# Graph attention and mixture-of-experts block on one core: new places in the instruction queues for the first softmax tiles, and a turn of 33 places

## The chip, the cores and the metric

The kernel runs on one NeuronCore of a Trainium2 chip. The metric is the device time of one execution in microseconds (us). Before the change the median of 3 runs is 1457.65 us (1455.25 to 1458.83); the execution that was profiled took 1455.44 us, of which the span from its first to its last instruction is 1453.6 us.

## The reference

The reference adds to a node table x (1250 x 768, float32) first a two-layer graph attention network of layernorm(x), then a transformer block with 12-head attention and a top-2 mixture of 8 experts. The change lies in graph attention layer 1:

```python
h = x @ W
e_src = h @ a_src
e_dst = h @ a_dst
e = leaky_relu(e_src[src] + e_dst[dst], 0.2)
m = segment_max(e, dst)
w = exp(e - m[dst])
z = segment_sum(w, dst)
out = segment_sum(h[src] * (w / z[dst])[:, None], dst) + b      # then relu, then layer 2
```

There are 41,250 edges (20,000 drawn, each in both directions, and the 1250 self-loops), sorted by dst.

## The kernel before

**Dense form of the graph.** The 1250 nodes are T = 10 tiles of 125. For each destination tile the kernel counts how many edges run from each source to each destination (a 125 x 1250 table `cnt`), and the segment sums become matrix products. The counts come from one-hot matrices: 38 steps per tile, 380 in all. In step g TensorE multiplies a destination one-hot by a source one-hot (`step_near`, L1960). VectorE makes the source one-hots in batches of 4 steps (2 at a tile's end; `ohs`, L2403) and the destination one-hots in batches of 12 or 14 (`ohd`, L2337); ScalarE scales each destination one-hot by a packed power (`valued`, L2102). After 38 steps ScalarE copies the counts out (`counted`, L2089) and VectorE unpacks them (`unpacked`, L2416). Steps of the next tile that use the same PSUM bank wait for that copy.

**Layer 1's products.** For each tile t, in float32 split into high and low parts: transpose (`transposes1`, L1914), ScalarE's high part (`higher1`, L2072), VectorE's low part (`lower1`, L2363), twelve triples of matrix products (`triple1`, L457 to L459), the result's high part (`result1` on ScalarE, L2083), the scores (`score1` on VectorE, L2374) and the result's low part (`rest1`, L2379). The source scores go through DRAM to be spread over all partitions (`esb`): the first 8 tiles' scores in one transfer, the last 2 tiles' in a second.

**The softmax of tile t.** ScalarE turns the counts into a mask (`distant`, L863). VectorE takes the masked maximum (`far_max`, L880; for tile 0 in two parts, L903), forms the shift (`shift_sum` L885, `shift` L889) and adds and clips the scores (`leaky`, L896; for tile 0 in two parts, L900). ScalarE's `sloped1` (L800) makes the 0.2-scaled scores `es02` that the clip reads, in the same two parts. ScalarE takes the exponential (`exponential`, L849), VectorE multiplies by the counts (`weigh`, L909), TensorE transposes (`turned`, L811), ScalarE copies out the high part (`higher`, L854, L855), VectorE the low part (`lower`, L914, L915), and TensorE does 20 triples (`triple_sum`, L457 to L459). `ending` (L919, L2388) divides and adds the bias.

**The order is written out.** Every engine takes its instructions strictly in its own queue's order. The queue of layer 1 is made on each engine by one loop over places g = 0 to SCHEDULE - 1; a part is put into the queue at the place that a formula names. Place g also holds counting step g while g < 380, so a place is a common clock for the three queues, but only semaphores tie them. Products of tile t have place `linear(t, r)`, 14 places per tile. Softmax parts and sums have place `turn_at(k, x)`: turn k begins at TURN0 + TURN * k and is cut in 21 slots; turns before 0 are 12 places long. Tile t's sums lie in turn t, its softmax in turns t - 1 and t - 2. The count copies have places 38, 76, 114, 152 and so on (`counted_at`). Within one place ScalarE's loop puts the count copy first, then the values, the product parts, `sloped1`, then `higher` and `exponential`.

After 380 the queues hold the last tiles' softmax and sums alone, and the splits of layer 2's weights (`weights2`, L2094, L632). Then follow layer 2, the attention (from about 500 us) and the experts.

For the prediction's steps, the places before the change are these. ScalarE: `sloped1` part 0 at 113, count copy 2 at 114, result of tile 7 at 115, `higher1` of tile 9 at 116, `sloped1` part 1 at 124, exponential of tile 0 at 130, tile 6 at 303, count copy 7 at 304. VectorE: first part of tile 0's maximum and clip (`SHIFT_AT[0]`) at 115, source one-hots of steps 118 to 121 at 118, unpack 2 and score of tile 7 at 122, low parts of tile 7's result and tile 9's input at 124, second part at 127, tile 0's weighting at 132, the score of tile 8 at 136, its low part and tile 0's `lower` at 138, tile 1's maximum at 139 and clip at 141, tile 6's weighting at 308. TensorE: tile 9's products at 126 to 137, tile 0's transposes at 133, its first sum at 143.

Of the kernel before, what the change touches and what calls it, by code (L numbers as in the profile page):

```python
# [9 lines left out]
T = N // P  # L10
# [45 lines left out]
SRC_BATCHES = -(-WINDOW // SRC_WIDE)  # L56
STEPS = T * WINDOW
FIRST, PERIOD, PARTS = 0, 14, 13
TURN0, TURN, EARLY, SLOTS = FIRST + 142, 32, 12, 21
AHEAD = 20  # L60
COUNT_READY = 8
MOMENTS_DVE = tuple(range(0, T, 2))
# [13 lines left out]
def linear(t, r):  # L76
    return FIRST + PERIOD * (PARTS * t + r) // PARTS


def turn_at(k, x):  # L80
    return TURN0 + (TURN * k + TURN * x // SLOTS if k >= 0 else EARLY * k + EARLY * x // SLOTS)
# [5 lines left out]
WEIGHT1_AT = (5, 6, 9, 10, 11, 13)  # L87
PRODUCT_AT = (linear(0, 12), linear(1, 2), linear(1, 14), linear(2, 6), linear(2, 18), linear(3, 10))
ROW_AT = dict(zip(range(ROWS_FROM, T), (linear(4, 16), linear(5, 8), linear(5, 14), linear(6, 14), linear(7, 7))))
SLOPED_AT = (linear(7, 14), linear(8, 12))  # L90
SHIFT_AT = (linear(7, 16), linear(8, 14))


def digits_until(g):
    return min(g + min(AHEAD, 8 + g), STEPS)
# [10 lines left out]
def counted_at(j):  # L106
    return WINDOW * (j + 1)
# [48 lines left out]
def build(nc, x, src, dst, gw1, gas1, gad1, gb1, gw2, gas2, gad2, gb2,  # L156
# [241 lines left out]
    with ctx:  # L398
# [3 lines left out]
        def sem(name):  # L402
            if name not in sems:
                sems[name] = ctx.enter_context(nc.semaphore(name))
            return sems[name]
# [1488 lines left out]
        def _(pe):  # L1894
# [12 lines left out]
            def transposes1(t):  # L1907
                pe.wait_ge(sem("h1_row"), t + 1)
                pe.wait_ge(sem("tile_lo"), t + 2)
                if t in SOURCES_AT:  # L1910
                    source_turned1(pe, SOURCES_AT.index(t))
                for k in range(KD):
                    at = k // 3 * BANK + k % 3 * P
                    last = pe.transpose(ps[:, at:at + P], tin[:, t % 2, k * 128:(k + 1) * 128], ident[0:P, 0:P])  # L1914
                last.then_inc(sem("tile_raw"), 1)
# [32 lines left out]
            def step_near(g):  # L1948

                j, u = divmod(g, WINDOW)  # L1950
                b, i = src_batch(g)
                into = bank(count_bank(j), P, PACK)
                if u == 0:
                    before = [i for i in range(j) if count_bank(i) == count_bank(j)]
                    if before:
                        pe.wait_ge(sem("cnt_read"), before[-1] + 1)
                if i == 0:
                    pe.wait_ge(sem("oh_ready"), b + 1)
                pe.wait_ge(sem("valued"), g + 1)
                pe.matmul(into, hot_dst(g), hot_src(g), start=u == 0, stop=u == WINDOW - 1).then_inc(sem("oh_free"), 1)  # L1960
                if u == WINDOW // 2:
                    c = P * j // DIGITS
                    width = min(SELF, PACK - c)
                    pe.matmul(bank(count_bank(j), P, c + width)[:, c:c + width], identb[:, :], selfw[:, P * j % DIGITS, 0:width],
                              start=False, stop=False)

            def tile_all(j):

                pe.wait_ge(sem("cnt_read"), j + 1)
                for h in range(DIGITS):  # L1970
                    c = DIGITS * j + h
                    if c:
                        pe.wait_ge(sem("block_read"), c)

                    def turn(r, first, last):
                        for u in range(8):
                            pe.wait_ge(sem("ohg_ready"), r * 8 + (ALL_STEPS * c + u + 1))
                            pe.matmul(bank(3, P, PACK), ohdg[:, u % 4, :], ohsg[:, u % 4, :],
                                      start=first and u == 0, stop=last and u == 7).then_inc(sem("ohg_free"), 1)
                    turn(0, True, False)  # L1980
                    with pe.Fori(1, ALL_STEPS // 8 - 1) as r:
                        turn(r, False, False)
                    turn(ALL_STEPS // 8 - 1, False, True)

            def first_layer(near):

                for g in range(SCHEDULE):
                    if near and g < STEPS:
                        step_near(g)
                    for j in range(T):  # L1990
                        if not near and g == counted_at(j) + COUNT_READY:
                            tile_all(j)
                    for t in range(T):
                        if t and g == linear(t - 1, 6 if t == 1 else 0):
                            transposes1(t)
                        for i in range(2 * KD):
                            if g == linear(t, i):
                                triple1(t, i)
                    for t in range(T):
                        if g == turn_at(t - 1, 6):  # L2000
                            turned(pe, 0, t, t % 2)
                    if g == turn_at(T - 1, 6):
                        transposes2(pe, 0)
                    for t in range(T):
                        for i in range(2 * T):
                            if g == turn_at(t, i + 1):
                                if t == 0 and i in (0, T - 1):
                                    pe.wait_ge(sem("tile_yfree"), T + 1 + (i > 0))
                                triple_sum(pe, 0, t, t % 2, i)
# [23 lines left out]
        def _(act):  # L2033
# [106 lines left out]
            for g in range(SCHEDULE):  # L2140
                for j in range(T):
                    if g == counted_at(j):
                        counted(j)
                for q in range(digits_until(g), digits_until(g + 1)):
                    valued(q)
                for t in range(T):
                    if t >= 2 and g == max(linear(t - 3, 6), 4 * t - 4):
                        if t in MOMENTS_DVE:
                            root1(t)
                        else:  # L2150
                            moments1(t)
                            rooted1(t)
                    if t and g == linear(t - 1, 9 if t == 1 else 4):
                        higher1(t)
                    if t >= 2 and g == max(linear(t - 2, 9 if t < T - 1 else 3), 10):
                        normed(t)
                    if g == linear(t, 16):
                        result1(t)
                if g in SLOPED_AT:
                    sloped1(act, SLOPED_AT.index(g))  # L2160
                if g == EXP_LOAD:
                    act.activation(stat[:, 0, 0:1], viol[0:P, 3:4], ACT.Exp)
                for t in range(T):
                    if g == turn_at(t - 1, 9):
                        higher(act, 0, t)
                    if g == turn_at(t - 1, 1):
                        exponential(act, 0, t)
                    if g == max(turn_at(t - 3, 16) if t else 0, counted_at(t) + COUNT_READY + 1):
                        distant(act, 0, t)
                for k in range(KD):  # L2170
                    if g == weight2_at(k):
                        weights2(k)
                if g == turn_at(T - 1, 9):
                    higher2(act, 0)
# [142 lines left out]
        def _(dve):  # L2317
# [125 lines left out]
            def first_layer(near):  # L2443

                for g in range(SCHEDULE):
# [24 lines left out]
                    for t in range(T):  # L2470
# [12 lines left out]
                        if t >= ROWS_FROM and g == ROW_AT[t]:  # L2483
                            row_score1(dve, t)
                    if g == SHIFT_AT[0]:
                        slopes1(dve, order, 0, ROWS_FROM)
# [6 lines left out]
                    if g == linear(T - 1, 19) + 1:  # L2493
                        slopes1(dve, order, ROWS_FROM, T)
                    if g == SHIFT_AT[1]:
                        dve.wait_ge(sem("src_moved"), 96)
# [5 lines left out]
                        dve.wait_ge(sem("agg_sl"), 2)  # L2502
                        leaky_part(dve, EARLY_ES, N).then_inc(sem("agg_l"), 1)
                    for t in range(T):
                        if t and g == turn_at(t - 2, 16):
                            far_max(dve, order, 0, t)
                        if t and g == turn_at(t - 2, 18):
                            shift_sum(dve, order, 0, t)
                        if t and g == turn_at(t - 2, 19):
                            shift(dve, order, 0, t)  # L2510
                        if t and g == turn_at(t - 2, 20):
                            leaky(dve, 0, t)
                        if g == turn_at(t + 1, 9):
                            ending(dve, order, 0, t, finish1)
                        if g == turn_at(t - 1, 15):
                            lower(dve, 0, t)
                        if g == turn_at(t - 1, 4):
                            weigh(dve, 0, t)
                    for k in range(KD):
                        if g == weight2_low_at(k):  # L2520
# [241 lines left out]
            tiles, cum, first, limit = (ecol[:, c, :] for c in range(4))  # L2762
# [153 lines left out]
```

## Time and profile before

| | us |
|---|---|
| median of 3 runs | 1457.65 (1455.25 to 1458.83) |
| profiled execution | 1455.44 |
| its span | 1453.6 |
| TensorE busy, matmul | 1371.6 (94%) |
| TensorE busy, weight loads | 1311.7 (90%) |
| VectorE busy | 1136.0 (78%) |
| ScalarE busy | 910.6 (63%) |
| GpSimd busy | 442.3 (30%) |

A busy share is an average over stages. The stage of this change is the first fifth of the span. In the timeline views a row is one instruction, or several alike in succession: start, duration, engine and line, what is written and read, how many, and in brackets the idle time before it and what ended that. Instructions overlap by their pipeline's fill, so what one costs its queue is the distance from its start to the next one's start, which is shorter than its duration; the prediction calls that the pitch. PE is TensorE, DVE is VectorE, ACT is ScalarE.

### The profile page before, as it was taken

The page shows a single profiled execution, that of the slowest core. Times are in us where ns is not written, and L with a number is a line of the kernel's source. Part 1 is how long each engine was busy: PE and PEld are TensorE (multiplying, and loading weights), DVE is VectorE, ACT ScalarE, POOL GpSimd, SP SyncE. Part 2 cuts the span into 40 slices and gives each one's busy share as a digit, 9 for nine tenths or more (in the row PEclk, how much of TensorE's full clock was granted, in tenths as well). Part 3 has the DMA queues.
Part 4 walks back from the last instruction along what each step waited for, and adds up shares of the span by engine and source line. Part 5 has one row for each costly group of instructions (what it writes and reads, how often), then busy time and mean ns, then how long its engine had stood idle before and what let it go on. Part 6 is the DMA issues. An engine that isn't in the chain of part 4 may idle for free.

```text
span 1453.6 us, 25503 instructions
## 1 busy us (share of the span) xinstructions
PE 1371.6 (94%) x8947; PEld 1311.7 (90%) x8947; DVE 1136.0 (78%) x1553; ACT 910.6 (63%) x1607; POOL 442.3 (30%) x336
## 2 busy tenths in 40 slices
PE   3998999999999999899999999999998999899997
PEld 3887889999999998899999999999998997799996
DVE  5999999646997533768868778788687888888885
ACT  7887777333674320748668478485787411799995
POOL 1000000000000010626546357364477400455563
PEclk9999999999999999999999999999999999999999
DMA  8001000221445500000000000000011496467641
GB/s 212 2 26 47 22 22 22 91 103 40 146 143 170 175 6 23 1 1 23 1 0 22 0 22 0 0 22 0 0 44 52 129 315 161 121 165 179 157 102 19
DMA packets 49070, 101.18 MB, mean 70 GB/s; under 512 B 7268, under 2 KB 23106, under 8 KB 48984
## 3 DMA queue, kind: packets, MB, share of 16 engines
q1 hardware_dynamic: 40795, 76.02, 16.7%
q0 software_dynamic: 7488, 22.26, 7.5%
q10 hardware_dynamic: 701, 1.79, 0.4%
q8 instruction: 49, 0.80, 0.2%
q14 instruction: 37, 0.30, 0.1%
HBM read 69.22 MB, written 33.71 MB: 71 GB/s over the span
## 4 chain that ended last, share of the span: by engine, by line
PE 67%; DVE 5%; issue 3%; DMA 2%; ACT 2%; POOL 1%; ACTq 0%; POOLq 0%; SPq 0%; DVEq 0%
PE ps L457 13%; PE ps L458 13%; PE ps L459 13%; PE ps L1026 5%; PE ps L1071 4%; PE ps L1073 4%; PE ps L1072 4%; PE ps L1050 4%; PE ps L1052 4%; PE ps L1495 1%; POOL prlo L1258 1%; DVE mcol L1295 1%; PE ps L811 1%; DVE prlo L1258 1%; DMA hin<-hid_d 1%
## 5 line engine op out<-in xcount | busy, mean ns | idle before, releaser
L1258 POOL TENSOR_TENSOR prlo<-prob,prhi 125x500 fp32r<-125x500 f32 x180 | 258.7, 1444 | 250.8 <-ACT prob L1196 250.2
L1295 DVE TENSOR_REDUCE mcol<-ps 125x1 f32<-125x1250 f32 x120 | 174.9, 1458 | 73.6 <-PE ps L1026 72.1
L1194 ACT ACTIVATE prhi<-ps 125x500 fp32r<-125x500 f32 x300 | 176.7, 589 | 71.4 <-PE ps L1052 64.7
L1071 PE MATMUL ps<-prhi,vhi 125*128 125x250 f32 x600 | 172.0, 287 | 12.6 <-POOL prlo L1258 8.3
L1196 ACT ACTIVATE prob<-ps 125x500 f32<-125x500 f32 x300 | 176.4, 588 | 1.7 <-DVE prlo L1258 1.7
L1073 PE MATMUL ps<-prlo,vhi 125*128 125x250 f32 x600 | 168.4, 281 | 0.0
L1072 PE MATMUL ps<-prhi,vlo 125*64 125x250 f32 x600 | 167.4, 279 | 0.0
L1050 PE MATMUL ps<-qst,kst 128*125 128x250 f32 x600 | 155.9, 283 | 3.1 <-issue 1.3
L1052 PE MATMUL ps<-q,k 128*125 128x250 f32 x600 | 153.7, 280 | 0.0
L457 PE MATMUL ps<-hhi,pthl 125*125 125x384 f32 x400 | 153.4, 383 | 0.0
L1802 POOL MEMSET q<- 128x2500 f32 x1 | 2.2, 2187 | 472.4 <-PE ps L459 472.4
L1258 DVE TENSOR_TENSOR prlo<-prob,prhi 125x500 fp32r<-125x500 f32 x120 | 104.6, 872 | 49.4 <-ACT prob L1196 48.0
L458 PE MATMUL ps<-hhi,pthl 125*125 125x384 f32 x400 | 135.3, 338 | 0.0
L459 PE MATMUL ps<-hlo,pthl 125*125 125x384 f32 x400 | 135.1, 338 | 0.0
L1071 PEld LDWEIGHTS ps<-prhi,vhi 125*128 125x128 f32 x600 | 114.3, 191 | 18.1 <-issue 7.6
L2102 ACT ACTIVATE ohd<-ohd,sval 128x125 bf16<-128x125 bf16 x380 | 120.1, 427 | 0.6 <-DVE ohd L2337 0.6
L1050 PEld LDWEIGHTS ps<-qst,kst 128*125 128x125 f32 x600 | 112.5, 188 | 8.3 <-issue 1.5
L1960 PE MATMUL ps<-ohs,ohd 128*125 128x313 bf16 x380 | 101.3, 311 | 13.9 <-DVE ohs L2403 11.1
L1073 PEld LDWEIGHTS ps<-prlo,vhi 125*128 125x128 f32 x600 | 113.8, 190 | 0.0
L1052 PEld LDWEIGHTS ps<-q,k 128*125 128x125 f32 x600 | 112.9, 188 | 0.0
L1026 PE MATMUL ps<-kst,qst 128*125 128x512 f32 x360 | 93.2, 367 | 3.7 <-DVE mcol L1295 2.6
L457 PE MATMUL ps<-whi,txhi 128*125 128x384 f32 x228 | 89.8, 394 | 0.0
(365 smaller groups left out, 3856.2 us busy)
## 6 DMA issues: line engine op xcount, KB each, us to landing
w1all<-in_L_ffn_W_dram SPq DMA_DIRECT2D x8, 1152.0 KB, 12.0
w2st<-in_L_ffn_W_dram SPq DMA_DIRECT2D x8, 1152.0 KB
wqst<-in_L_ffn_Wqkv_dram SPq DMA_DIRECT2D x12, 384.0 KB, 4.2
hid_d<-tin SPq DMA_DIRECT2D x10, 375.0 KB
hin<-hid_d SPq DMA_DIRECT2D x10, 375.0 KB
vtin<-xn_d SPq DMA_DIRECT2D x10, 375.0 KB
out_dram<-accr POOLq DMA_DIRECT2D x10, 375.0 KB, 8.0
xres<-in_x_dram SPq DMA_DIRECT2D x10, 336.0 KB
```

The lines of the kernel that those rows point to most:

```text
L457: pe.matmul(o, lhi, rhi, start=start, stop=False)
L458: pe.matmul(o, llo, rhi, start=False, stop=False)
L459: return pe.matmul(o, lhi, rlo, start=False, stop=stop)
L1050: pe.matmul(o, kst[:, e, kt * P:(kt + 1) * P], qst[:, e, g * GQ:(g + 1) * GQ], start=True, stop=False)
L1052: last = pe.matmul(o, k2[:, e, kt * P:(kt + 1) * P], q2[:, e, g * GQ:(g + 1) * GQ], start=False, stop=True)
L1071: pe.matmul(ps[:, b:b + GQ], vhi[:, e, kt, :], hi, start=kt == 0, stop=False)
L1072: pe.matmul(ps[0:HD, b:b + GQ], vlo[:, e, kt, :], hi, start=False, stop=False)
L1073: last = pe.matmul(ps[:, b:b + GQ], vhi[:, e, kt, :], lo, start=False, stop=kt == T - 1)
L1194: act.activation(prhi[:, n % RING, :], bank(3 + n % 3, P, 2 * GQ), ACT.Exp, scale=float(HD) ** -0.5)
L1196: act.activation(prob[:, n % 3, :], bank(3 + n % 3, P, 2 * GQ), ACT.Exp, scale=float(HD) ** -0.5)\
L1258: eng.tensor_tensor(prlo[:, n % RING, :], prob[:, n % 3, :], prhi[:, n % RING, :].bitcast(f32), ALU.subtract)\
L1295: dve.tensor_reduce(mcol[:, e, t:t + 1], ps[0:P, 0:N], AX.X, ALU.max, negate=True).then_inc(sem("max"), 1)
```

## The change

It changes no instruction and no count of instructions, only places.

- `TURN0` goes from 142 to 138 and `TURN` from 32 to 33. Turn k begins at 138 + 33k, before at 142 + 32k. Turn 4 begins at 270 in both; turn 0 begins 4 places earlier, turn 7 3 places later.
- `sloped1` goes from places 113 and 124 to 117 and 127; tile 0's two parts of maximum and clip from 115 and 127 to 121 and 129.
- The parts of tiles 0 and 1 get places of their own. Tile 0: exponential 129, weighting 131, transposes 133, high part 134, low part 136. Tile 1: maximum 133, shift 134 and 135, clip 143, exponential 144, weighting 149, transposes 153, high part 156, low part 161. Before, tile 1's maximum stood behind tile 0's low part; now it stands ahead of it.
- Tile 0's first sum goes from 143 to 139, its second from 145 to 141.
- By the new turn, tile 6's exponential goes from 303 to 304 and its weighting from 308 to 309.
- SyncE's and GpSimd's queues have no places and stay as they are.

```diff
-TURN0, TURN, EARLY, SLOTS = FIRST + 142, 32, 12, 21
+TURN0, TURN, EARLY, SLOTS = FIRST + 138, 33, 12, 21
...
-SLOPED_AT = (linear(7, 14), linear(8, 12))
-SHIFT_AT = (linear(7, 16), linear(8, 14))
+SLOPED_AT = (linear(7, 18), linear(8, 14))
+SHIFT_AT = (linear(7, 22), linear(8, 16))
+
+def softmax_at(x, first, second=None):
+    return tuple(linear(T - 1, first) if t == 0 else turn_at(*second) if t == 1 and second else turn_at(t - 1, x) for t in range(T))
+
+EXP_AT, WEIGH_AT = softmax_at(1, 3, (0, 4)), softmax_at(4, 5, (0, 7))
+TURNED_AT, HIGHER_AT, LOWER_AT = softmax_at(6, 7, (0, 10)), softmax_at(9, 8, (0, 12)), softmax_at(15, 10)
+FAR_AT, SUM_AT, LESS_AT, LEAKY_AT = (tuple(linear(T - 1, first) if t == 1 else turn_at(t - 2, x) for t in range(T))
+                                     for x, first in ((16, 7), (18, 8), (19, 9), (20, 16)))
...
-                        if g == turn_at(t - 1, 6):
+                        if g == TURNED_AT[t]:
                             turned(pe, 0, t, t % 2)
...
-                    if g == turn_at(t - 1, 9):
+                    if g == HIGHER_AT[t]:
                         higher(act, 0, t)
-                    if g == turn_at(t - 1, 1):
+                    if g == EXP_AT[t]:
                         exponential(act, 0, t)
...
-                        if t and g == turn_at(t - 2, 16):
+                        if t and g == FAR_AT[t]:
                             far_max(dve, order, 0, t)
-                        if t and g == turn_at(t - 2, 18):
+                        if t and g == SUM_AT[t]:
                             shift_sum(dve, order, 0, t)
-                        if t and g == turn_at(t - 2, 19):
+                        if t and g == LESS_AT[t]:
                             shift(dve, order, 0, t)
-                        if t and g == turn_at(t - 2, 20):
+                        if t and g == LEAKY_AT[t]:
                             leaky(dve, 0, t)
...
-                        if g == turn_at(t - 1, 15):
+                        if g == LOWER_AT[t]:
                             lower(dve, 0, t)
-                        if g == turn_at(t - 1, 4):
+                        if g == WEIGH_AT[t]:
                             weigh(dve, 0, t)
```

## Rows read from the trace of the kernel before

**Rows 1.** The page's first part: busy time, share of the span, instructions.

```profile
PE 1371.6 (94%) x8947; PEld 1311.7 (90%) x8947; DVE 1136.0 (78%) x1553; ACT 910.6 (63%) x1607; POOL 442.3 (30%) x336
```

**Rows 2.** Busy time by stretch: the counting turns together, and turns 3 and 4.

```profile
122.85:259.70 136.85, 129.68 (x800) 119.61 (x800) 126.75 (x203) 99.09 (x264) 0.00 (x0) 0.99 0.11 32
172.21:189.90 17.69, 16.91 (x105) 15.10 (x104) 16.90 (x29) 13.51 (x37) 0.00 (x0) 1.00 0.07 22
189.90:207.11 17.21, 16.65 (x104) 15.29 (x103) 16.28 (x27) 12.35 (x34) 0.00 (x0) 1.00 0.08 23
```

**Rows 3.** TensorE's timeline from 107 us to the first sum.

```profile
107.14 0.31 PE L1960 MATMUL ps<-ohs,ohd 128*125 128x313 bf16 x1
...
109.06 0.36 PE L1960 MATMUL ps<-ohs,ohd 128*125 128x313 bf16 x1 [1.09 <-ACT packed L2089]
...
122.85 1.25 PE L811 MATMUL ps<-ident,lg 125*125 125x125 f32 x10
...
127.75 0.78 PE L1960 MATMUL ps<-ohs,ohd 128*125 128x313 bf16 x4 [0.97 <-DVE ohs L2403]
132.59 0.79 PE L1960 MATMUL ps<-ohs,ohd 128*125 128x313 bf16 x2 [4.06 <-DVE ohs L2403]
132.98 0.72 PE L457 MATMUL ps<-hhi,pthl 125*125 125x384 f32 x1
```

**Rows 4.** TensorE's timeline in turn 1 (starts of three successive sums).

```profile
169.79 0.45 PE L457 MATMUL ps<-hhi,pthl 125*125 125x384 f32 x1
...
170.61 0.46 PE L457 MATMUL ps<-hhi,pthl 125*125 125x384 f32 x1
...
171.29 0.45 PE L457 MATMUL ps<-hhi,pthl 125*125 125x384 f32 x1
```

**Rows 5.** ScalarE's timeline from 107 to 112 us, whole.

```profile
107.65 1.04 ACT L800 ACTIVATE es<-esb 125x1000 f32<-125x1000 f32 x1 [2.97 <-DMA esb<-es_d]
108.59 0.41 ACT L2089 ACTIVATE packed<-ps 125x313 int32<-125x313 f32 x1
108.90 0.72 ACT L2102 ACTIVATE ohd<-ohd,sval 128x125 bf16<-128x125 bf16 x2
109.48 0.79 ACT L2083 ACTIVATE hhi<-ps 125x768 fp32r<-125x768 f32 x1
110.17 0.43 ACT L2102 ACTIVATE ohd<-ohd,sval 128x125 bf16<-128x125 bf16 x1
110.46 0.25 ACT L763 ACTIVATE srow<-ps 2x125 f32<-2x125 f32 x1
110.62 0.77 ACT L2072 ACTIVATE txhi<-ps 128x750 fp32r<-128x750 f32 x1
111.30 2.46 ACT L2102 ACTIVATE ohd<-ohd,sval 128x125 bf16<-128x125 bf16 x8
```

**Rows 6.** VectorE's timeline from 107 to 128 us.

```profile
107.75 1.20 DVE L903 CUSTOM_DVE_ANT_0 far<-esb,far 125x1000 bf16<-125x1000 f32 x1 [2.32 <-DMA esb<-es_d]
...
108.88 1.25 DVE L900 SCALAR_TENSOR_TENSOR lg<-esb,ed,es 125x1000 f32<-125x1000 f32 x1
110.05 0.80 DVE L2403 TENSOR_TENSOR ohs<-iota,scodd 128x1252 bf16<-128x1252 f16 x1
110.77 1.61 DVE L2416 TENSOR_SCALAR cnt<-packed 125x313 uint16<-125x313 uint16 x4
112.16 0.99 DVE L2374 SCALAR_TENSOR_TENSOR row<-ps,att 125x768 f32<-125x768 f32 x1
...
125.45 1.20 DVE L914 TENSOR_TENSOR pthl<-ps,pthl 125x1000 fp32r<-125x1000 f32 x1 [1.44 <-ACT pthl L855]
```

**Rows 7.** Both engines' timeline around place 304.

```profile
217.44 1.34 ACT L849 ACTIVATE lg<-lg,zsum 125x1250 f32<-125x1250 f32 x1 [1.93 <-DVE lg L896]
...
219.38 1.45 DVE L909 SCALAR_TENSOR_TENSOR lg<-lg,cnt 125x1250 f32<-125x1250 f32 x1
...
219.80 0.43 ACT L2089 ACTIVATE packed<-ps 125x313 int32<-125x313 f32 x1 [1.02 <-PE ps L1960]
```

**Rows 8.** Busy time in 1 us; the eighth value is the granted clock's share.

```profile
133.00:134.00 1.00, 1.00 (x5) 1.00 (x4) 1.00 (x3) 1.00 (x5) 0.00 (x0) 0.50 0.00 0
136.00:137.00 1.00, 1.00 (x8) 0.96 (x7) 1.00 (x2) 0.00 (x0) 0.00 (x0) 1.00 0.85 194
```

**Rows 9.** TensorE's idle time after the last count.

```profile
269.81 1.35 PE L811 MATMUL ps<-ident,lg 125*125 125x125 f32 x10 [1.10 <-DVE lg L909]
```

## The prediction

> **What bounds the kernel now.** I read the page's busy shares first. They name TensorE: 94% by matmuls, 90% by weight loads, VectorE 78% [rows 1]. For the stage of the change that is misleading, so next I read busy time by stretch. While the counting runs, 122.85 to 259.70 us, VectorE is busy 126.75 of 136.85 us (93%), TensorE's weight loads 119.61 (87%) [rows 2]. A turn there takes 17.2 to 17.7 us, with VectorE busy 16.3 to 16.9 of it.
>
> What TensorE itself needs of a turn comes from the timeline. Two sums with one counting step between start 0.68 us apart, with two steps 0.82 us [rows 4]: a step is 0.14, a triple 0.54. Twenty triples and 32 steps are 10.8 + 4.5, the ten transposes 1.0: 16.3 us. So both engines run close to full, VectorE a little closer, and each waits on the other through the one-hots. Then I read the timelines around the first sum. TensorE idles 0.97 and 4.06 us there, each time for source one-hots that VectorE makes late [rows 3]. VectorE in its turn idled 2.32 us for the scores and 1.44 us for tile 0's high part [rows 6]. The change aims at these four gaps. Its worth is what it does to VectorE's idle time before the last count, for VectorE's work up to there is the same in both kernels.
>
> **Part 1: `sloped1` and the first shift part later.** Removed: ScalarE's 2.97 us wait for the scores ahead of count copy 2 [rows 5], and with it TensorE's 1.09 us wait for that copy [rows 3]. The last count of tile 2 starts at 107.14 and takes 0.31, so the copy starts at 107.5 and the next count at 107.9, before 109.06.
>
> Added: `sloped1` now stands behind work that it was ahead of. By pitches of [rows 5]: count copy 0.31, two values 0.58, result 0.69, value 0.29, source row 0.16, `higher1` 0.68, one more value 0.29. From 107.5 that is 110.5; `sloped1`'s own 0.94 makes 111.45, and VectorE sees it at about 111.6 (0.15 us from one engine's end to the other's start; [rows 6]: 125.45 follows a copy that left its queue at 125.30).
>
> VectorE's maximum part still has to wait for the scores until 107.75, since the transfer doesn't move; what changes is that the one-hots of steps 118 to 121 (pitch 0.72) are made inside that wait. It ends at 108.88 as before. Then the clip (`leaky_part`), which followed at once before, waits for `sloped1`: 111.6 - 108.9 = 2.7 us. It ends at 112.8, before at 110.05, and the 0.72 already done makes VectorE 2.0 us late from here on. **This new wait takes the place of the one removed.** Queued behind it are the unpack (1.39), the score (0.91) and the one-hots of step 122 (0.72): these are there at 115.8. TensorE, now early, would be at step 122 at 107.9 + 8 x 0.665 = 113.3 and waits 2.6; step 126 needs the low parts (0.87 + 0.84), destination one-hots (0.85) and 0.72 more, 119.1, and costs another 1.8. The last product ends near 128.7, before near 126.6.
>
> **Part 2: the chain of tiles 0 and 1.** From 119.1 on VectorE does the second shift part (1.4) and a batch of one-hots until 121.3. The exponential follows the shift, 120.5 + 0.14 + 1.24, so weighting starts at 122.1 and ends at 123.5. Now the maximum and shift sum of tile 1 (1.67) fill the wait for tile 0's high part; a batch (0.72), 0.1 and a score (0.89) bring VectorE to 126.85. The high part comes at 127.4 (transposes at 124.8, copy 1.2, hand-overs 0.4), so 0.5 us is idle where it was 1.44. Low part 1.44, rest 0.87, batch 0.72: 130.4. The first sum starts near 130.8, before at 132.98 [rows 3]: **2.2 us earlier, and the 4.06 us gap of TensorE is gone** (1.9 us before step 138 in its place). But VectorE, which had 2.0 us to make up, has made up only 0.9. I carried the same walk over the old order to check the pitches: it meets the trace within 0.5 us at the tile transposes of 154, 172, 190, 207 and 240 us. At place 152 the new order is 1.1 us behind the old.
>
> Bounds of parts 1 and 2: with the copy, values and result free of waits, `sloped1` can't end before 111.4; if TensorE's records are 0.3 late it is 111.1, and the loss 0.8. If the scores land 1 us later, the old kernel loses that whole us and the new one nothing, which makes the sum 0.1. Landing 1 us earlier makes it 2.1.
>
> **Part 3: the clock.** In the microsecond after the 4.06 us gap the granted clock is 0.50 (1.2 GHz), and at 136 it is 1.00 again [rows 8]; so it is down for some 3 us, in which TensorE does the work of 1.5 us. The old walk takes no notice of it and is right again by 154 us, because VectorE bounds; put in, it moves the old kernel by 0.4. Gain 0.4, between 0 and 1.5.
>
> By the Trainium skill, page "TensorE: Matmul & The Clock Gate", section "HAM oscillation", idle gaps between bursts of matmuls put the array back to half rate, and the penalty is half of the throttled time. The trace agrees with the drop behind the 4.06 us gap. The rule speaks against the change too: part 1 opens gaps of 2.6 and 1.8 us with 1.6 us of work between. By it the sum could lose a second such penalty; that is the third rival.
>
> **Part 4: a turn of 33 places.** Each tile's sums stand one place further behind for each turn. Up to place 302 VectorE loses another 0.6 us to this, in waits of 0.3 to 1 us that shift about (bounds 0 and 1.2). At place 304 there is a sharp one. Before, tile 6's exponential (place 303) was ahead of count copy 7 (304), so VectorE could weight at 219.38 while ScalarE idled 1.02 us for the last count, copying at 219.80 [rows 7]. Now both are at 304 and the copy comes first. Exponential and weighting wait for the last count of tile 7: 219.8 + 1.7 behind by then gives 221.5; copy 0.31, a value 0.29, exponential 1.24, hand-overs 0.45: 223.8. VectorE would be ready at 221.75 and idles 2.1. Of this 0.7 is had back from waits that the old order has at the same batches; 1.4 stays (bounds 0 and 2.1).
>
> After the last count TensorE alone bounds. Turn 7 begins at 369, before 366, so 147 of the 200 sums, before 149, stand ahead of step 380. The two more cost 1.08, but cover the 1.10 us that TensorE idles for tile 9's weighting [rows 9]; the walk gives 0.2 (bounds 0 and 1.1). Behind that everything starts later by the same amount: layer 2, attention and experts have no place in the change.
>
> **Sum:** +1.1 +0.6 +1.4 +0.2 -0.4 = +2.9 us. On the profiled execution's 1455.44 us that is 1458.3 us; that execution lies 2.2 under the median, so on the median it is 1460.5 us.
>
> **Rivals.**
>
> *Nothing left of it.* VectorE's waits at 304 and in the drift are covered, because the waits of this stretch fall differently by 0.5 us at every batch, and the head's 1.1 less 0.4 is all: +0.7, 1458.4 us. For it: its terms are worked out far from the place where I can check them. Against: the copy ahead of the exponential is a fact of the order.
>
> *Faster: TensorE is the bound.* If TensorE, not VectorE, limits the turns, what counts is its idle time at the first sum. It loses 0.97 + 4.06 us of gaps [rows 3] and 1.5 of half clock, and gets 1.1 of later sums: -5.4, 1452.2 us. It decides from the point at which the clip finds `sloped1` done, for then VectorE is 2.0 earlier and keeps ahead. For it: 94% against 78% over the whole span [rows 1]. Against: 93% against 87% in the stretch [rows 2], and the 2.7 us of part 1. By the Trainium skill, "Perfetto Trace Analysis", section "Identifying the Most-Contended Engine", other engines are judged by occupancy and TensorE by its weight loads; over the span this names TensorE, and in the stretch VectorE.
>
> *The clock falls earlier.* The two gaps of part 1 lead to a stretch at 1.2 GHz during tile 9's products: 1.5 us more, as every instruction there is ahead of tile 1's clip. +4.4, 1462.0 us. For it: TensorE would work 1.6 us of 6 from 113.3 to 119.2. Against: no single gap is as long as 4.06.
>
> **How the numbers follow.** Forecast 0.50 (its own range 1458.5 to 1463), nothing left 0.24, clock 0.14, faster 0.12. The range holds the first three and the spread of about 2 us in the runs shown: 1455 to 1465.5. A measurement of this kernel tells some 0.3% (4.4 us) from no change. Slower by more: half of the clock case, and a third of the forecast, where the 304 wait comes at its full 2.1 and the drift at 1.2: 0.23. Faster by more: 0.11, nearly all of the fourth case. Within: 0.66.
>
> **What would show it.** Right: VectorE's row of L900 waits 2 to 3 us for ScalarE's L800 near 111.5; TensorE waits for one-hots near 113 to 119; the first sum starts near 131; no clock under 1.00 from 125 to 140; ScalarE's count copy near 221.8 stands ahead of the exponential, with VectorE's weighting waiting 1 us or more; the last count is 2 to 4 us later than 259.7. Wrong: no wait at L900, or a last count that comes before 259.7. If the last count is late and the total is not, something in layer 2 took it back, and I have missed a slack.

## The result: 0.33% slower, and the profile after

| | before | after |
|---|---|---|
| median of 12 runs, us | 1455.86 (1454.52 to 1458.83) | 1461.01 (1458.14 to 1463.73) |
| ratio | | 1.0033, 95% interval 1.0023 to 1.0043 |
| profiled execution's span, us | 1453.6 | 1460.9 |

In time the ratio is +4.8 us (3.3 to 6.3): small, but clear of no change. Forecast was a loss of 2.9 us. The lines of the new kernel are 11 higher than before from the softmax functions on: L911 is the former L900, L811 the former `sloped1` L800, L822 the transposes, L860 the exponential, L920 the weighting, L2100 the count copy, L1971 the counting step.

First the page and the counting stretch by busy time, beside [rows 1, 2]. The second fence is the answer by stretch. Its columns: stretch, length, busy us (and instructions) of PE, of the weight loads, of DVE, ACT and GpSimd, then the granted clock's share, the share of the DMA engines, GB/s.

```profile
PE 1377.4 (94%) x8947; PEld 1315.8 (90%) x8947; DVE 1131.2 (77%) x1553; ACT 911.0 (62%) x1607; POOL 437.0 (30%) x336
```

```profile
117.00:118.00 1.00, 1.00 (x5) 0.90 (x4) 1.00 (x2) 0.00 (x0) 0.00 (x0) 0.50 0.00 0
...
125.07:263.03 137.96, 127.79 (x795) 117.26 (x795) 126.89 (x202) 98.53 (x264) 0.00 (x0) 1.00 0.10 31
133.00:134.00 1.00, 1.00 (x8) 0.92 (x8) 1.00 (x2) 0.19 (x1) 0.00 (x0) 1.00 0.00 0
```

VectorE's work in the stretch is the same, 126.9 us. The clock is no longer halved at 133 us as in [rows 8], but it is at 117, behind the new gap. Now VectorE's timeline, beside [rows 6]:

```profile
106.09 0.81 DVE L2414 TENSOR_TENSOR ohs<-iota,scodd 128x1252 bf16<-128x1252 f16 x1 [0.56 <-PE ps L1971]
...
107.17 1.20 DVE L914 CUSTOM_DVE_ANT_0 far<-esb,far 125x1000 bf16<-125x1000 f32 x1 [0.18 <-DVE ed L756]
...
111.70 1.26 DVE L911 SCALAR_TENSOR_TENSOR lg<-esb,ed,es 125x1000 f32<-125x1000 f32 x1 [3.33 <-ACT es L811]
112.88 1.60 DVE L2427 TENSOR_SCALAR cnt<-packed 125x313 uint16<-125x313 uint16 x4
```

and ScalarE's, beside [rows 5]:

```profile
107.64 0.43 ACT L2100 ACTIVATE packed<-ps 125x313 int32<-125x313 f32 x1 [2.79 <-PE ps L1971]
107.97 0.72 ACT L2113 ACTIVATE ohd<-ohd,sval 128x125 bf16<-128x125 bf16 x2
...
109.68 0.77 ACT L2083 ACTIVATE txhi<-ps 128x750 fp32r<-128x750 f32 x1
110.36 0.42 ACT L2113 ACTIVATE ohd<-ohd,sval 128x125 bf16<-128x125 bf16 x1
110.65 1.02 ACT L811 ACTIVATE es<-esb 125x1000 f32<-125x1000 f32 x1
```

VectorE's 2.32 us wait for the scores is gone, and right behind the maximum, at the clip, a wait of 3.33 us for ScalarE has come. `sloped1` starts 3.0 us after the count copy, since the whole block from the copy to `higher1` is ahead of it. TensorE's timeline, beside [rows 3]:

```profile
116.05 0.36 PE L1971 MATMUL ps<-ohs,ohd 128*125 128x313 bf16 x1 [2.40 <-DVE ohs L2414]
...
119.46 0.45 PE L1971 MATMUL ps<-ohs,ohd 128*125 128x313 bf16 x1 [0.35 <-DVE ohs L2414]
...
130.83 0.50 PE L1971 MATMUL ps<-ohs,ohd 128*125 128x313 bf16 x2 [1.84 <-DVE ohs L2414]
131.05 0.45 PE L468 MATMUL ps<-hhi,pthl 125*125 125x384 f32 x1
```

The first sum is 1.9 us earlier (131.05, before 132.98) and the 4.06 us gap has become 1.84. All of TensorE's gaps from 108 us to the first sum add up to 4.59 us; before they were 7.26. And at place 304, both engines in two answers, beside [rows 7]:

```profile
221.69 0.43 ACT L2100 ACTIVATE packed<-ps 125x313 int32<-125x313 f32 x1 [4.60 <-PE ps L1971]
222.02 0.43 ACT L2113 ACTIVATE ohd<-ohd,sval 128x125 bf16<-128x125 bf16 x1
222.31 1.33 ACT L860 ACTIVATE lg<-lg,zsum 125x1250 f32<-125x1250 f32 x1
```

```profile
223.67 1.46 DVE L920 SCALAR_TENSOR_TENSOR lg<-lg,cnt 125x1250 f32<-125x1250 f32 x1 [1.98 <-ACT lg L860]
```

The copy stands ahead of the exponential, ScalarE is idle 4.60 us before it, and VectorE 1.98 us behind both.

### The profile page after: what moved, and what is told of

The parts are those of the page before. It is cut to its first block, busy times and chain, and to the rows that moved or that the text cites. A ratio compares the mean times of both kernels' runs of the same rounds, so it can differ in the third digit from the quotient of the medians.

```text
span 1460.9 us, 25503 instructions
## 1 busy us (share of the span) xinstructions
PE 1377.4 (94%) x8947; PEld 1315.8 (90%) x8947; DVE 1131.2 (77%) x1553; ACT 911.0 (62%) x1607; POOL 437.0 (30%) x336
## 4 chain that ended last, share of the span: by engine, by line
PE 66%; DVE 5%; DMA 3%; issue 3%; ACT 2%; POOL 1%; SPq 0%; POOLq 0%; ACTq 0%; DVEq 0%
PE ps L468 12%; PE ps L469 12%; PE ps L470 12%; PE ps L1037 5%; PE ps L1082 4%; PE ps L1084 4%; PE ps L1083 4%; PE ps L1061 4%; PE ps L1063 4%; PE ps L1506 1%; POOL prlo L1269 1%; DMA hin<-hid_d 1%; DVE mcol L1306 1%; DVE prlo L1269 1%; PE ps L822 1%
## 5 line engine op out<-in xcount | busy, mean ns | idle before, releaser
L1269 DVE TENSOR_TENSOR prlo<-prob,prhi 125x500 fp32r<-125x500 f32 x120 | 98.9, 824 | 49.4 <-ACT prob L1207 48.0
L1971 PE MATMUL ps<-ohs,ohd 128*125 128x313 bf16 x380 | 101.2, 311 | 17.1 <-DVE ohs L2414 12.9
```

Source lines behind the costliest of these rows:

```text
L1269: eng.tensor_tensor(prlo[:, n % RING, :], prob[:, n % 3, :], prhi[:, n % RING, :].bitcast(f32), ALU.subtract)\
```

## The experiments

Each is a whole kernel, timed beside the kernel before. Two measures are given: the ratio, and from the profiled execution the shift of the first transposes of layer 2 against the kernel before (281.53 us), which marks the end of layer 1. The second is taken against a transposition of tile 8 at 97.49 us, ahead of every edit, to take out a different start of the trace (up to 0.3 us). By it the changed kernel is **+3.1 us**; the walk had said +3.3. The walk is the calculation of the prediction: all three queues gone through in order, with measured pitches and the waits between them, the clock left out.

| kernel | walk | trace, end of layer 1 | total, us (95%) |
|---|---|---|---|
| changed kernel | +3.3 | +3.1 | +4.8 (3.3 to 6.3) |
| e1_slope_early | +0.5 | -0.1 | -0.9 (-3.1 to 1.5) |
| e2_scores_only | +2.0 | +2.1 | +3.3 (1.3 to 5.4) |
| e3_exp_ahead | +1.95 | +1.6 | +3.3 (1.2 to 5.4) |
| e4_turn_137 | -2.6 | -2.9 | -2.5 (-4.4 to -0.4) |
| e5_pe_more | +2.8 | +2.7 | +2.0 (-0.6 to 4.7) |
| e6_dve_more | +1.8 | +2.1 | +0.6 (-1.7 to 3.1) |
| e7_pe_late | +3.2 | +3.8 | -2.3 (-4.2 to -0.6) |
| e8_warm | -0.4 | -0.3 | -1.3 (-3.2 to 0.6) |
| e9_chain_only | +0.4 | +0.4 | +1.7 (0 to 3.5) |
| e10_scores_back | +1.3 | +0.75 | +2.6 (0.7 to 4.5) |
| e11_tuned | -4.6 | -5.4 | -4.7 (-6.7 to -2.8) |
| e12_all_later | +3.2 | +3.5 | +2.2 (0.3 to 4.1) |

The totals are the ratios and their intervals times 1456 us.

The same shift can be read on the way, at ScalarE's count copies. The columns are their places (in the kernel before at 108.59, 138.42, 158.73, 219.80 and 239.25 us):

| kernel | 114 | 152 | 190 | 304 | 342 | end of layer 1 |
|---|---|---|---|---|---|---|
| changed kernel | -1.1 | -0.2 | +2.1 | +1.7 | +3.1 | +3.1 |
| e2_scores_only | -1.1 | +2.1 | +2.1 | +2.1 | +2.1 | +2.1 |
| e3_exp_ahead | -1.1 | +0.1 | +1.95 | +1.6 | +1.55 | +1.6 |
| e5_pe_more | -0.45 | -0.3 | +0.3 | +1.0 | +2.0 | +2.7 |
| e6_dve_more | -0.25 | +0.05 | 0.0 | +0.45 | +2.0 | +2.1 |
| e7_pe_late | -0.3 | +0.6 | +0.55 | +0.5 | +0.5 | +3.8 |
| e8_warm | -0.25 | -1.8 | -0.2 | -0.25 | -0.3 | -0.3 |
| e9_chain_only | +0.1 | -2.4 | +0.5 | +0.4 | +0.4 | +0.4 |
| e10_scores_back | -0.2 | -2.5 | -0.2 | -0.6 | +0.7 | +0.75 |
| e12_all_later | +3.0 | +3.6 | +3.6 | +3.5 | +3.5 | +3.5 |

It also shows how far a mark can be trusted. e5 to e8 differ from the kernel before only behind place 114, yet stand 0.25 to 0.45 us early there, because their scores landed that much sooner in the profiled execution; e7, which differs only behind the last count, is 0.5 us late by place 342. A mark of one profile carries some 0.5 us of this.

**e1_slope_early.** In the changed kernel:

```diff
-SLOPED_AT = (linear(7, 18), linear(8, 14))
+SLOPED_AT = (linear(7, 14), linear(8, 14))
```

> The changed kernel with sloped1's first part back at place 113 (all else as changed). If the new wait of VectorE's clip for ScalarE's sloped1 is what part 1 costs (the queues' walk): the 3.3 us gap ahead of L911 is gone, the last count of tile 9 is 2.8 us earlier than in the changed kernel and the total 2.8 us lower, +0.5 us on the kernel before. If TensorE's idle time bounds the stretch and the cost comes from the turn of 33 places alone: the gap goes but the total stays within 1 us of the changed kernel's.

VectorE's timeline of this kernel at the same place:

```profile
107.38 1.20 DVE L914 CUSTOM_DVE_ANT_0 far<-esb,far 125x1000 bf16<-125x1000 f32 x1 [0.48 <-DMA esb<-es_d]
...
108.50 1.25 DVE L911 SCALAR_TENSOR_TENSOR lg<-esb,ed,es 125x1000 f32<-125x1000 f32 x1
109.67 1.64 DVE L2427 TENSOR_SCALAR cnt<-packed 125x313 uint16<-125x313 uint16 x4
```

No gap ahead of L911. Moving this one instruction in ScalarE's queue takes 3.2 us off the end of layer 1, 0.4 of it because the scores landed sooner here, and no loss is left that the runs could tell (median 1456.28, before 1456.37). The new wait is what part 1 costs; the rival in which it moves nothing falls.

**e2_scores_only and e10_scores_back**, the same edit by itself, and everything but it. In the kernel before, and the reverse in the changed one:

```diff
-SLOPED_AT = (linear(7, 14), linear(8, 12))
-SHIFT_AT = (linear(7, 16), linear(8, 14))
+SLOPED_AT = (linear(7, 18), linear(8, 14))
+SHIFT_AT = (linear(7, 22), linear(8, 16))
```

> The kernel before with only sloped1 and the two shift parts moved later (117 and 127; 121 and 129), old chain and old turn. By the walk: +2.0 us in the last count and in the total, all from the new wait of VectorE at its clip. By the rival (TensorE bounds): the copy of the counts comes 1.1 us sooner for TensorE, the total is the same or lower.

> The changed kernel with sloped1 and the shift parts at their old places; the chain and the turn (138, 33) stay. By the walk: last count +1.1, end of layer 1's sums +1.3 on the kernel before, 2.0 less than the changed kernel; the total +1.3. If the new wait isn't what costs: as the changed kernel, +3.3 in the trace.

VectorE's timeline of e2:

```profile
107.52 1.20 DVE L903 CUSTOM_DVE_ANT_0 far<-esb,far 125x1000 bf16<-125x1000 f32 x1 [0.58 <-DMA esb<-es_d]
...
111.65 1.26 DVE L900 SCALAR_TENSOR_TENSOR lg<-esb,ed,es 125x1000 f32<-125x1000 f32 x1 [2.93 <-ACT es L800]
```

TensorE's timeline and a microsecond by stretch, for the question of the clock:

```profile
115.97 0.36 PE L1960 MATMUL ps<-ohs,ohd 128*125 128x313 bf16 x1 [2.36 <-DVE ohs L2403]
...
119.38 0.35 PE L1960 MATMUL ps<-ohs,ohd 128*125 128x313 bf16 x1 [1.58 <-DVE ohs L2403]
```

```profile
117.00:118.00 1.00, 0.80 (x5) 0.46 (x4) 1.00 (x2) 0.45 (x1) 0.00 (x0) 1.00 0.00 0
```

The edit alone makes the end of layer 1 2.1 us later and the total 3.3; without it the changed kernel is 2.3 us earlier there. Both ways it is some 2 us, and by the table e2 has them from place 152 on unchanged. Chain and turn together are not free either: +0.75. By the table they are 0.6 us ahead at place 304 and lose 1.3 between there and 342, where tile 6's exponential waits behind the count copy.

**e3_exp_ahead.** In the changed kernel, tile 6's exponential at 303:

```diff
+EXP_AT = tuple(g - 1 if t == 6 else g for t, g in enumerate(EXP_AT))
```

> The changed kernel with tile 6's exponential one place earlier (303), ahead of count copy 7. By the walk: VectorE's 2.0 us wait ahead of tile 6's weighting goes, the last count and the total are 1.35 us earlier than in the changed kernel (+1.95 on the kernel before). If that wait is covered by others (rival: the drift comes of the turn's length alone): no change, within 0.3 us in the trace at the last count.

ScalarE's, then VectorE's timeline of this kernel:

```profile
218.45 1.34 ACT L861 ACTIVATE lg<-lg,zsum 125x1250 f32<-125x1250 f32 x1 [1.73 <-DVE lg L908]
221.32 0.43 ACT L2101 ACTIVATE packed<-ps 125x313 int32<-125x313 f32 x1 [1.53 <-PE ps L1972]
```

```profile
220.51 0.81 DVE L2415 TENSOR_TENSOR ohs<-iota,scol 128x1252 bf16<-128x1252 f16 x1
221.23 1.46 DVE L921 SCALAR_TENSOR_TENSOR lg<-lg,cnt 125x1250 f32<-125x1250 f32 x1
```

The weighting no longer waits, and layer 1 ends 1.5 us earlier than in the changed kernel; by the table the two part behind place 304. That is one place for one instruction. In the totals the 1.5 us lie inside the interval.

**e4_turn_137 and e11_tuned**, versions meant to beat both. e4 is e1 with `TURN0` 137; e11 adds four places that the walk picked:

```diff
-TURN0, TURN, EARLY, SLOTS = FIRST + 138, 33, 12, 21
+TURN0, TURN, EARLY, SLOTS = FIRST + 137, 33, 12, 21
...
-SLOPED_AT = (linear(7, 18), linear(8, 14))
+SLOPED_AT = (linear(7, 14), linear(8, 14))
...
-EXP_AT, WEIGH_AT = softmax_at(1, 3, (0, 4)), softmax_at(4, 5, (0, 7))
-TURNED_AT, HIGHER_AT, LOWER_AT = softmax_at(6, 7, (0, 10)), softmax_at(9, 8, (0, 12)), softmax_at(15, 10)
+EXP_AT, WEIGH_AT = softmax_at(1, 3, (0, 4)), softmax_at(4, 8, (0, 7))
+TURNED_AT, HIGHER_AT, LOWER_AT = softmax_at(6, 6, (0, 9)), softmax_at(9, 8, (0, 12)), softmax_at(15, 12)
```

> The changed kernel with TURN0 137 in place of 138 and sloped1's first part at 113. All turns stand one place earlier, which also puts tile 6's exponential (303) ahead of count copy 7. By the walk: last count 2.8 us and end of layer 1's sums 2.6 us earlier than in the kernel before, total -2.6 us, faster than both. By the rival that order effects of single places are noise: like e1, +0.5 us.

> The changed kernel with TURN0 137, sloped1's first part at 113, tile 0's weighting at linear(9, 8), its transposes at linear(9, 6), its low part at linear(9, 12) and tile 1's transposes at slot 9. Chosen by the walk: last count 4.8, end of layer 1's sums 4.6 us earlier than in the kernel before; total -4.6, 2 us under the version with TURN0 137 alone. If the walk's fine structure means nothing: like that one, -2.5.

e4: median 1453.98 beside 1456.37, ratio 0.9983 (0.9970 to 0.9997). e11: 1450.41 beside 1455.89, ratio 0.9968 (0.9954 to 0.9981): **faster than both**, layer 1 ends 5.4 us earlier than before. All of VectorE's waits over 0.3 us between the shift parts and the last count, from its timeline in e11:

```profile
153.59 0.81 DVE L2414 TENSOR_TENSOR ohs<-iota,scodd 128x1252 bf16<-128x1252 f16 x1 [0.91 <-PE ps L1971]
...
199.16 1.46 DVE L920 SCALAR_TENSOR_TENSOR lg<-lg,cnt 125x1250 f32<-125x1250 f32 x1 [0.44 <-ACT lg L860]
...
205.35 0.81 DVE L2414 TENSOR_TENSOR ohs<-iota,scol 128x1252 bf16<-128x1252 f16 x1 [0.39 <-PE ps L1971]
```

They are 1.7 us in all, where the changed kernel has 1.98 in one.

**e9_chain_only.** The changed kernel with `TURN0, TURN` 142, 32 and the old `SLOPED_AT` and `SHIFT_AT`.

> The changed kernel with the old turn (142, 32) and sloped1 and the shift parts at their old places: only tile 0's and 1's own chain places are new. By the walk VectorE is 0.9 us ahead at place 152, loses that by tile 3's sums, last count +0.4, total +0.4. By the rival that the earlier first sum is kept to the end: -0.9 to -2.3.

The first sum is 2.5 us earlier, the end of layer 1 0.4 us later. The lead of the earlier first sum is gone by the copy at place 190, 28 us behind it. Set against e10, which has the same chain and the new turn, this kernel is 1.0 us later at place 304: up to there the turn of 33 costs nothing. The new turn without the new chain wasn't tried.

**e5_pe_more and e6_dve_more**, which engine bounds. In the kernel before, the first in `triple_sum` ahead of a tile's first triple, the second in `finish1`:

```diff
+                if n == 0 and 1 <= t <= 7:
+                    keep_busy(pe, 4 + 2 * u, 3)
```

```diff
+                if t < 6:
+                    order.did(dve.scalar_tensor_tensor(halves(tin[:, u, :]), two(4 + 2 * u, P, HALF), zsum[:, u, 5:6],
+                                                       halves(brow[:, :]), ALU.mult, ALU.add))
+                    order.wait()
```

> The kernel before with 3 more matrix products (128x512 bf16, written to the sums' bank before its first sum, about 0.65 us) at each of turns 1 to 7, 4.5 us of added TensorE work, all but the last turn's ahead of the last count. If VectorE alone bounds the counting stretch, nearly all of it hides but turn 7's, under 1 us. If TensorE alone bounds it: +4.5. The walk of all three queues says neither: +2.8.

> The kernel before with tiles 0 to 5's last VectorE instruction of layer 1 (L2388) done twice, 6 times 1.0 us of added VectorE work, all ahead of the last count. If VectorE alone bounds: +6. If TensorE alone bounds: about 0. The walk: the added work falls largely into waits that VectorE has there anyway, +1.8.

Neither engine bounds alone. Of 4.5 us of TensorE's work 2.7 come through (3.0 counted from place 152, ahead of the first addition), of 6 us of VectorE's 2.1. By stretch, e5 and then e6:

```profile
122.38:262.30 139.92, 133.61 (x821) 122.48 (x821) 127.20 (x203) 99.25 (x264) 0.00 (x0) 0.98 0.11 31
```

```profile
122.53:261.70 139.17, 130.68 (x800) 119.79 (x800) 132.68 (x209) 99.24 (x264) 0.00 (x0) 0.98 0.11 31
```

Against [rows 2], TensorE's busy time is up by 3.9 and the stretch by 3.1; VectorE's by 5.9 and the stretch by 2.3. Added work fills waits that were there. The later clip of e2 comes through whole: VectorE's next one-hots are 1.9 us later, the end of layer 1 2.1.

**e8_warm.** In the kernel before, ahead of TensorE's 4 us gap:

```diff
+                        if t == 0 and g == 141:
+                            pe.wait_ge(sem("tile_yfree"), T + 1)
+                            keep_busy(pe, 4, 14)
```

> The kernel before with 14 matrix products (3 us) put into TensorE's 4 us gap ahead of step 142. The granted clock stays at 1.00 from 132 to 136 us. By the walk the half clock behind the gap is worth 0.4 us at the last count. By the rival (TensorE bounds the turns) it is worth its whole 1.5 us.

By stretch, 132 to 136 us of this kernel:

```profile
132.00:136.00 4.00, 3.57 (x22) 3.36 (x23) 4.00 (x9) 3.39 (x9) 0.00 (x0) 1.00 0.40 77
```

The clock stays at 1.00, and the end of layer 1 comes 0.3 us earlier, not 1.5. But this kernel is 0.25 us early already at place 114, ahead of the edit, for its scores landed 0.25 us sooner (2.07 us of wait in place of 2.32). By the table the full clock brings 1.5 us at place 152, and all of it is gone at 190. So the half clock of the kernel before cost nothing that a mark could tell. In e7, whose code is the same here, the clock is down for longer:

```profile
136.00:137.00 1.00, 1.00 (x5) 0.87 (x5) 1.00 (x2) 0.00 (x0) 0.00 (x0) 0.50 0.87 289
```

It is 1.00 there in the kernel before [rows 8]. e7 falls back by 0.8 us between places 114 and 152, and keeps it to the last count.

**e7_pe_late and e12_all_later**, is a later start dear further on? In the kernel before:

```diff
+                if n == 0 and t == T - 1:
+                    keep_busy(pe, 4 + 2 * u, 15)
```

```diff
+            for i in range(3 if n == 0 else 0):
+                act.activation(es02[:, a:b], esb[:, a:b], ACT.Copy, scale=SLOPE).then_inc(sem("sl_more"), 1)
+                act.wait_ge(sem("sl_more"), i + 1)
             act.activation(es02[:, a:b], esb[:, a:b], ACT.Copy, scale=SLOPE).then_inc(sem("agg_sl"), 1)
```

> The kernel before with 15 more matrix products on TensorE ahead of tile 9's sums, after the last count, where TensorE alone works: 3.2 us. It delays layer 2 and all that follows as the change does, without touching the order. If what follows only moves: +3.2 in the trace at layer 2's start and in the total. If a later start costs something of its own further on (rival: half-clock stretches in the attention and projection stages that come or go by when they start): total +4.5 to +5.

> The kernel before with sloped1's first part done four times in succession, each waiting for the one before: some 3.2 us during which all three queues stand, and nothing else changed. The end of layer 1 is 3.2 us later. If what follows only moves, the total is +3.2. If a later start costs more further on (the changed kernel shows +4.8 in the total and +3.3 at that point), it is +4.5 to +5.

Layer 2 starts 3.8 and 3.5 us later, the totals are -2.3 and +2.2 us. So no price of a later start shows (e12's interval ends at 4.1). In e7, 0.5 us of the 3.8 were there before the added products. e7 isn't a clean delay either: only TensorE stood, the transfers of layer 2's first rows did not, and the 1.68 us wait for one of them at 313.64 us in the kernel before isn't there. Its trace is 3.6 us behind ahead of that place and 2.2 at 357 us. The rest of e7's total I can't account for.

## Why the prediction was right

The measured time, 1461.01 us, is 0.5 us from the forecast 1460.5, but that closeness is luck: the median of the kernel before was 1457.65 in three runs and is 1455.86 in twelve, so the base was 1.8 us too high, and the loss is 4.8 us, where 2.9 was the sum. A loss of more than 0.3% had been given a chance of 0.23. What held is the direction and the mechanism up to the end of layer 1, but for the clock and the cause of the drift.

- *Part 1, the new wait.* 2.7 us forecast, 3.33 in the trace, with the maximum starting 0.6 us sooner than assumed; the clip starts at 111.70, forecast 111.6. VectorE's one-hots of step 122 are 1.95 us late, forecast 2.0. Shown by e2 and e10: worth 2.1 and 2.3 us.
- *Part 2, the chain.* First sum forecast at 130.8, measured 131.05. Step 122 at 115.8, measured 116.05. VectorE 1.1 us behind ahead of place 152, measured 1.08. That the earlier sum doesn't last is shown by e9.
- *Part 3, the clock.* 0.4 us forecast; e8 shows nothing beyond the 0.25 us that it had ahead of the edit. This term was too large; without it the sum is 3.3.
- *Part 4, the turn.* The place 304 wait forecast 2.1, measured 1.98, and 1.4 of it net; the changed kernel loses 1.35 between places 304 and 342, and e3 gets 1.5 back. The drift of 0.6 up to place 302 has the right size (1.08 us behind at 152 on VectorE, 1.73 at 304) and the wrong cause: e9, with the old turn, goes from 0.9 us ahead to 0.4 behind, so the longer turn is not what loses it. What does is open. After the last count the forecast was 0.2, measured 0.0.
- *The sum.* Layer 1 ends 3.1 us later; the forecast of its terms was 3.3 less 0.4 of clock. The 1.7 us up to the measured 4.8 have no term in the prediction.
- *"VectorE a little closer" to the bound.* This step was only half right. e6 shows that VectorE's work alone comes through to a third. The forecast came through all the same, since its terms were waits of one queue on another, not busy time.
- *The faster rival* had a price that rests on TensorE's idle time. That time did fall, by 2.7 us, the first sum did come 1.9 us sooner, and the kernel is slower. The price was also wrong by its own rule: it counted the gaps that close and left out the 2.6 and 1.8 us that part 1 opens, with which -5.4 would have been -1.0.
- *Nothing left of it* fell at place 304: the wait is there, and e3 shows that it isn't covered.
- *The clock rival* came true as an event (0.50 at 117 us) and failed as a price. TensorE was waiting for one-hots at that moment anyway: the second gap, forecast 1.8 us, is 0.35 in the trace, and the slow products fill the rest. e2 has the two gaps with a clock of 1.00 all along (its rows above), and tile 0's transposes are 1.9 us later there than before; in the changed kernel, with the half clock, they are 2.1 us later. So the half clock cost at most 0.2 us.

**What stays open** is the missing 1.7 us, the difference between a mark that carries some 0.5 us and a total whose interval begins at 3.3. The profiled execution shows where such time can lie. By stretch, the kernel before and then after; the eighth value is the clock:

```profile
1138.00:1144.00 6.00, 5.74 (x36) 5.57 (x35) 5.50 (x7) 0.00 (x0) 0.00 (x0) 1.00 0.04 16
1228.00:1238.00 10.00, 8.45 (x56) 4.23 (x56) 9.24 (x38) 0.40 (x1) 1.56 (x5) 1.00 0.51 132
```

```profile
1138.00:1144.00 6.00, 4.18 (x21) 3.74 (x19) 3.98 (x5) 2.46 (x4) 3.16 (x3) 0.72 0.16 64
1228.00:1238.00 10.00, 9.97 (x40) 5.92 (x41) 6.42 (x35) 2.10 (x4) 0.86 (x4) 0.66 0.19 43
```

In code that the change doesn't touch, at the end of the attention and in the routing, the clock is at 1.2 GHz for some us in one profile and not in the other. The span of this pair differs by 7.3 us. The changed kernel's trace is 3.1 us behind at the start of layer 2, 3.2 near the end of the attention (1134 us in the kernel before), 4.8 at the projection behind it (1139) and 6.8 at the experts' first tile (1243): 3.1 us come from layer 1, and 3.5 where the clock is down. In every kernel, time and mean clock of the timed runs go against each other (correlation -0.34 to -0.90), and single runs of one kernel spread over 4 to 10 us. Yet this doesn't explain the medians: the mean clock of the changed kernel's 12 runs is 0.990, as in 100 later runs of the kernel before, whose median is 1456.3. And e12, with a like delay, shows no such addition. So the runs show 3.1 us of the loss with its cause, and the rest without one.

## What to carry to other kernels

When a part is moved down a queue to spare a wait, look at what stands between its old and its new place, and at who waits for it: here `sloped1` moved four places on ScalarE, behind 2.7 us of work, and VectorE's next part waited for it. Where hand-made places are scaled by one number, check which instruction lands in the same place as a blocking one, since the order within the loop decides which goes first. And walk all queues together, with measured pitches and semaphores, instead of pricing the idle time of one engine: the gap that was aimed at shrank from 4.06 to 1.84 us, and the kernel became slower.

## What the runs showed of the hardware that was not expected

- Work added to an engine that is busy 93% of a stretch came through to 35% (2.1 of 6 us), less than on the one busy 87% by its weight loads (2.7 of 4.5). Busy share doesn't tell how much more fits in.
- Stretches at 1.2 GHz in which TensorE waited for VectorE's one-hots anyway had very different prices: nothing that a mark could tell in the kernel before (133 to 136 us), at most 0.2 us in the changed kernel (117 to 119 us), 0.8 us in e7, where it lasted until 137 us.
- One kernel's executions differ in where such stretches fall and in how long they last, and in time by several us. The landing of the scores differs as well, by 0.25 to 0.45 us between kernels with the same code up to there. Differences of 2 us are safer read from a mark in the trace than from 12 runs, where the edit lies in one stage: at the end of layer 1 the marks of the 12 experiments agree with the walk within 0.8 us; the totals are within 1.5 us of it, but e7's is 5.5 us off.
